# Attention of a diffusion block on one core: units of one key tile for two heads, sums in three of four banks, the bias table reloaded in place

## The reference

```
xn = ln(x, g_norm)
q  = l2norm((xn @ Wq) as 16 heads of 64) * q_scale
k, v = xn @ Wkv;  k = l2norm(k with the null key in front) * k_scale
sim = q @ k.T * 8 + bias[head, i - j]        # bias: a small MLP of the distance i - j
sim = causal mask(sim); attn = softmax(sim)  # the null key is always seen
y   = ln((attn @ v) as 1024 columns @ Wout, g_out)
x   = x + (round(y * 127 / max|y|) / (127 / max|y|)) @ W_ternary.T + bias
```

## Time and profile before

| | |
|---|---|
| time, median of 3 runs | 1911.69 us (1909.09 to 1911.83) |
| span of the profiled execution (its own time is not listed apart) | 1909.3 us |
| busy: PE, DVE, POOL, ACT, PEld | 1637.2, 1605.8, 1329.1, 1167.9, 1088.9 us |
| `score`, L1103, 2560 matmuls | 607.5 us |
| `weigh`, L1125, 8704 matmuls | 601.5 us |
| `bias`, L900, 640 | 697.3 us |
| low part, POOL L479, 448; DVE L910, 192 | 885.9 us; 292.1 us |
| exponential, ACT L611, 640 | 608.9 us |
| DMA | 69.49 MB, 36 GB/s over the span |

### The profile page before, as it was taken

The page is one execution under the profiler, slowest core; times in us unless marked ns, Lnnn a source line. Parts: engine busy times, 40 slices in busy tenths (PEclk is TensorE's granted clock), DMA queues, the critical chain, the costliest instruction groups (busy, mean ns, idle before and its releaser), DMA issues.

```text
span 1909.3 us, 46551 instructions
## 1 busy us (share of the span) xinstructions
PE 1637.2 (86%) x15098; PEld 1088.9 (57%) x15122; DVE 1605.8 (84%) x2569; ACT 1167.9 (61%) x2195; POOL 1329.1 (70%) x806
## 2 busy tenths in 40 slices
PE   3786996988988988988995887889889889889897
PEld 2343553666666666665552554666666666666553
DVE  5885996999999999996664898799999999999576
ACT  1433654777777777777441555677777777777542
POOL 3554675877777777777672676677777778778575
PEclk9997997999999999999997999899999999999998
DMA  5001110001001001000022001000100100100022
GB/s 174 1 0 26 28 56 20 25 24 47 23 26 44 23 31 39 23 23 11 28 71 91 28 27 58 25 25 23 47 23 23 47 23 23 47 23 0 12 72 94
DMA packets 28411, 69.49 MB, mean 36 GB/s; under 512 B 8368, under 2 KB 8880, under 8 KB 24240
## 3 DMA queue, kind: packets, MB, share of 16 engines
q1 hardware_dynamic: 23712, 60.22, 9.9%
q10 hardware_dynamic: 4640, 8.54, 1.3%
HBM read 60.21 MB, written 8.54 MB: 36 GB/s over the span
## 4 chain that ended last, share of the span: by engine, by line
PE 33%; issue 28%; DVE 19%; POOL 16%; DVEq 1%; POOLq 1%; ACT 0%; DMA 0%; ACTq 0%; SPq 0%
PE ps L1103 18%; PE ps L1125 14%; DVE work L900 10%; DVE work L910 6%; POOL rinv L458 3%; POOL work L463 3%; POOL work L490 3%; POOL qo L421 2%; POOL work L508 2%; PE ps L1161 1%; DVE work L926 1%; POOL rstd L453 1%; POOL work L466 1%; POOL work L429 1%; PE ps L1082 0%
## 5 line engine op out<-in xcount | busy, mean ns | idle before, releaser
L479 POOL TENSOR_TENSOR work<-work 128x1024 f16<-128x1024 f32 x448 | 885.9, 1997 | 267.2 <-ACT work L611 261.6
L611 ACT ACTIVATE work<-work 128x1024 f32<-128x1024 f32 (+1 forms) x640 | 608.9, 966 | 296.5 <-DVE work L900 296.4
L900 DVE SCALAR_TENSOR_TENSOR work<-ps,tab 128x1024 f32<-128x1024 f32 (+1 forms) x640 | 697.3, 1110 | 80.1 <-PE ps L1103 77.1
L1103 PE MATMUL ps<-qo,kT 128*128 (+1 forms) x2560 | 607.5, 360 | 115.9 <-DVE work L900 109.3
L1125 PEld LDWEIGHTS ps<-vals,work 128*128 128x128 bf16 (+1 forms) x8704 | 546.3, 98 | 128.8 <-ACT work L611 11.5
L1125 PE MATMUL ps<-vals,work 128*128 128x129 f16 x8704 | 601.5, 220 | 1.9 <-POOL work L479 1.9
L1103 PEld LDWEIGHTS ps<-qo,kT 128*128 128x128 f16 x2560 | 216.4, 98 | 273.2 <-DVE work L900 77.0
L910 DVE TENSOR_TENSOR work<-work 128x1024 f16<-128x1024 f32 x192 | 292.1, 1521 | 0.0
L1071 PE MATMUL ps<-wq,work 128*128 128x512 f16 x768 | 178.0, 390 | 20.5 <-DVE work L829 20.5
L1161 PE MATMUL ps<-wout,work 128*128 128x512 f16 x768 | 172.9, 382 | 0.0
L618 ACT ACTIVATE work<-null_v,p_null 128x65 f32<-128x65 f32 x512 | 135.2, 335 | 9.9 <-DVE work L931 9.9
(11 more groups left out here) (129 smaller groups left out, 1570.6 us busy)
## 6 DMA issues: line engine op xcount, KB each, us to landing
tab<-bias_table SPq DMA_DIRECT2D x32, 1088.0 KB, 5.6
work<-in_x SPq DMA_DIRECT2D x64, 256.0 KB, 2.7
out_x<-work ACTq DMA_DIRECT2D x32, 256.0 KB, 2.8
work<-in_L_cond_Wq SPq DMA_DIRECT2D x1, 2048.0 KB, 12.5
work<-in_L_cond_Wout SPq DMA_DIRECT2D x2, 1024.0 KB, 10.3
qo<-in_L_cond_w SPq DMA_DIRECT2D x1, 1024.0 KB, 8.7
qo<-in_L_cond_b SPq DMA_DIRECT2D x2, 256.0 KB, 4.2
qo<-in_L_cond_g SPq DMA_DIRECT2D x2, 256.0 KB, 4.5
```

Of the source, the lines that this page charges most:

```text
L479: pool.tensor_tensor(low[:, k % LRING, :, c0:512], probs[:, r, :, c0:512], high[:, r, :, c0:512], ALU.subtract).then_inc(low_pool, 1)
L611: act.activation(probs[:, k % RING, :, c0:512], probs[:, k % RING, :, c0:512], ACT.Exp).then_inc(expd, 1)
L900: dve.scalar_tensor_tensor(out=dst, in0=ps[:, 2 * (k % 2):2 * (k % 2) + 2, c0:512], scalar=SCORE, in1=t_ap, op0=ALU.mult, op1=ALU.add).the ...
L1103: last = pe.matmul(ps[:, 2 * (k % 2) + e, c0:512], kT[:, a, j * P:(j + 1) * P], qT[:, bass.ds(h, 1), 512 * i + c0:512 * i + 512].squeeze(1 ...
```

## The change

- A unit is now one key tile for *two heads* (`UNITS`, `unit`): 8 pairs of heads with 40 units, the blocks in the order 3, 2, 1, 0. On the diagonal a unit starts at the tile's own column: 512, 384, 256 and 128 columns. `score` has four matmuls again (two heads, keys' high and low halves); the low halves of odd heads' queries lie before the high ones (`q_part`), the products are all four as before.
- The sums of a block are eight tiles in three banks (3, 3 and 2 tiles), and the blocks go round four banks. A bank is drained as soon as its tiles are complete (`DONE`): q = 0 after the block's last but one unit, q = 1 and 2 after its last. The first `weigh` of a block waits separately for each bank.
- DVE takes 4 low parts of 40, POOL 36.
- `null_part` and `store_o` have eight small copies each, a block being that of two heads.
- The table of a pair of heads is held once; its quarter of 512 columns is loaded again after the block that was the last to use it, and `bias` waits at the units 0, 1, 5 and 9 (`NEARER`).
- PE's loop over heads becomes a written-out one over pairs. The output stage runs over the tiles from the last to the first, and its copy of `x` goes into the table's place.

```diff
-TW = S + P
+TW = S
+NEARER = (0, 1, 5, 9)
 ROUND = 1.5 * 2.0 ** 23
-PAIRS = [(i, q) for i in range(NB) for q in range(2 * i + 2)]
-NP = len(PAIRS)
+HP = H // 2
+BLOCKS = tuple(reversed(range(NB)))
+UNITS = [(i, j) for i in BLOCKS for j in range(4 * i + 4)]
+NU = len(UNITS)
...
-DVE_LOW = (2, 5, 8, 11, 14, 17)
-POOL_LOW = tuple(k for k in range(NP) if k not in DVE_LOW)
-LASTS = {PAIRS.index((i, 2 * i + 1)): i for i in range(NB)}
+DVE_LOW = (4, 10, 22, 32)
+POOL_LOW = tuple(k for k in range(NU) if k not in DVE_LOW)
+SUMS = 3
+SUM_TILES = (range(0, 3), range(3, 6), range(6, 8))
+LASTS = {UNITS.index((i, 4 * i + 3)): i for i in BLOCKS}
+NULLS = {UNITS.index((i, 4 * i + 1)): i for i in BLOCKS}
+DONE = {UNITS.index((i, 4 * i + 2)): (i, (0,)) for i in BLOCKS} | {
+    UNITS.index((i, 4 * i + 3)): (i, (1, 2)) for i in BLOCKS}
+def unit(k):
+    i, j = UNITS[k]
+    return i, j, P * max(0, j - 4 * i)
+def turn(i):
+    return NB - 1 - i
+def sum_bank(i, q):
+    return 4 + (SUMS * turn(i) + q) % 4
...
+        def q_part(u, low):
+            first = qhl[:, u, 0, 0:1]
+            return bass.AP(first.tensor, first.offset + (DH if low else 0),
+                           [first.ap[0], [2 * P, HP], [DH if low else 3 * DH, 2], [1, DH]])
...
-                with sp.Fori(0, H // 2) as h2:
-                    for u in range(2):
-                        h = h2 * 2 + u
-                        sp.wait_ge(biased, (b * H + h - 1) * NP + CB)
-                        sp.wait_ge(tab_ld, 16 * (b * H + h) + 16)
+                with sp.Fori(0, HP) as hp:
+                    for k, i in LASTS.items():
+                        sp.wait_ge(biased, (b * HP + hp - 1) * NU + k + 1 + CB)
+                        sp.wait_ge(tab_ld, 16 * ((b * HP + hp) * NB + turn(i)) + 16)
                         alone(sp)
-                        src = bass.AP(table.tensor, h * TABW + 1, [[1, P], [1, TW]])
-                        sp.dma_start(tab[:, u * TW:(u + 1) * TW], src).then_inc(tab_ld, 16)
-                sp.wait_ge(expd, (b + 1) * H * NP)
+                        src = bass.AP(table.tensor, hp * (2 * TABW) + 1 + P + 512 * i, [[1, P], [TABW, 2], [1, 512]])
+                        sp.dma_start(tab[:, :, 512 * i:512 * i + 512], src).then_inc(tab_ld, 16)
...
-                def null_part(h, i):
-                    n = (b * H + h) * NB + i
-                    act.wait_ge(o_added, n + 1)
-                    for s in range(4):
-                        last = act.activation(null_tmp[:, i % 2, s * VW:(s + 1) * VW], null_v[:, :], ACT.Copy,
-                                              scale=p_null[:, 4 * i + s, bass.ds(h, 1)])
+                def null_part(hp, i):
+                    m = (b * HP + hp) * NB + turn(i)
+                    act.wait_ge(o_added, 3 * m + 3)
+                    for t in range(8):
+                        last = act.activation(null_tmp[:, i % 2, t, :], null_v[:, :], ACT.Copy,
+                                              scale=p_null[:, 4 * i + t % 4, bass.ds(2 * hp + t // 4, 1)])
                     last.then_inc(null_ready, 1)
-                def store_o(h, i):
-                    n = (b * H + h) * NB + i
-                    act.wait_ge(o_rec, n + 1)
-                    act.wait_ge(o_added, n + 1 + 2)
-                    for s in range(4):
-                        last = act.activation(o_all[:, bass.ds(h, 1), 4 * i + s, :].squeeze(1),
-                                              o_sum[:, i % 2, s, :], ACT.Copy, scale=rec[:, i % 2, s:s + 1])
+                def store_o(hp, i):
+                    m = (b * HP + hp) * NB + turn(i)
+                    act.wait_ge(o_rec, m + 1)
+                    act.wait_ge(o_added, 3 * m + 3 + 6)
+                    for t in range(8):
+                        last = act.activation(o_all[:, bass.ds(2 * hp + t // 4, 1), 4 * i + t % 4, :].squeeze(1),
+                                              o_sum[:, i % 2, t, :], ACT.Copy, scale=rec[:, i % 2, t:t + 1])
                     last.then_inc(o_stored, 1)
...
-                def bias(h, k):
-                    n = (b * H + h) * NP + k
-                    i, q = PAIRS[k]
-                    c0 = 256 if k in LASTS else 0
-                    if k == 0:
-                        dve.wait_ge(tab_ld, 16 * (b * H + h + 1) + 16)
+                def bias(hp, k):
+                    n = (b * HP + hp) * NU + k
+                    i, j, c0 = unit(k)
+                    if i == BLOCKS[0] and j in NEARER:
+                        dve.wait_ge(tab_ld, 16 * ((b * HP + hp) * NB + NEARER.index(j) + 1) + 16)
                     dve.wait_ge(scored, n + 1)
                     dve.wait_ge(pv_done, n + 1)
-                    dst = probs[:, k % RING, :, c0:512]
-                    t_ap = tab[:, bass.ds((h % 2) * TW + (512 * i - 256 * q + c0), 2 * P)]
-                    t_ap = bass.AP(t_ap.tensor, t_ap.offset, [t_ap.ap[0], [P, 2], [1, 512 - c0]])
-                    dve.scalar_tensor_tensor(out=dst, in0=ps[:, 2 * (k % 2):2 * (k % 2) + 2, c0:512],
-                                             scalar=SCORE, in1=t_ap, op0=ALU.mult, op1=ALU.add
+                    x0 = 512 * i - P * j + c0
+                    dve.scalar_tensor_tensor(out=probs[:, k % RING, :, c0:512],
+                                             in0=ps[:, 2 * (k % 2):2 * (k % 2) + 2, c0:512], scalar=SCORE,
+                                             in1=tab[:, :, x0:x0 + 512 - c0], op0=ALU.mult, op1=ALU.add
                                              ).then_inc(biased, 1)
-                def low_part(h, k):
-                    n = (b * H + h) * NP + k
-                    c0 = 256 if k in LASTS else 0
+                def low_part(hp, k):
+                    n = (b * HP + hp) * NU + k
+                    i, j, c0 = unit(k)
                     r = k % RING
                     dve.wait_ge(expd, n + 1)
                     dve.wait_ge(pv_done, n + 1 + RING - LRING)
                     dve.tensor_tensor(low[:, k % LRING, :, c0:512], probs[:, r, :, c0:512], high[:, r, :, c0:512],
                                       ALU.subtract).then_inc(low_dve, 1)
-                def drain(h, i):
-                    n = (b * H + h) * NB + i
-                    last = PAIRS.index((i, 2 * i + 1))
-                    z = 4 + 2 * (i % 2)
-                    dve.wait_ge(pv_done, (b * H + h) * NP + last + 1 + RING)
-                    dve.wait_ge(null_ready, n + 1)
-                    dve.wait_ge(o_stored, n + 1)
-                    acc = ps[:, z:z + 2, 0:2 * VS].rearrange("p z (s d) -> p z s d", d=VS)
-                    null = null_tmp[:, i % 2, :].rearrange("p (z s d) -> p z s d", z=2, d=VW)
-                    part = o_part[:, i % 2, :, :].rearrange("p (z s) d -> p z s d", z=2)
-                    total = o_sum[:, i % 2, :, :].rearrange("p (z s) d -> p z s d", z=2)
-                    dve.tensor_tensor(denom[:, i % 2, :].rearrange("p (z s) -> p z s", z=2), acc[:, :, :, 2 * DH],
-                                      null[:, :, :, DH], ALU.add).then_inc(o_den, 1)
-                    dve.tensor_tensor(part, acc[:, :, :, DH:2 * DH], null[:, :, :, 0:DH], ALU.add
-                                      ).then_inc(o_low, 1)
-                    dve.wait_ge(o_den, n + 1)
-                    dve.reciprocal(rec[:, i % 2, :], denom[:, i % 2, :]).then_inc(o_rec, 1)
-                    dve.wait_ge(o_low, n + 1)
-                    dve.tensor_tensor(total, acc[:, :, :, 0:DH], part, ALU.add).then_inc(o_added, 1)
-                def head(h, first):
-                    for k in range(NP):
-                        bias(h, k)
+                def drain(hp, k):
+                    i, done = DONE[k]
+                    m = (b * HP + hp) * NB + turn(i)
+                    dve.wait_ge(pv_done, (b * HP + hp) * NU + k + 1 + RING)
+                    if 0 in done:
+                        dve.wait_ge(null_ready, m + 1)
+                        dve.wait_ge(o_stored, m + 1)
+                    for q in done:
+                        t0, n = SUM_TILES[q].start, len(SUM_TILES[q])
+                        acc = ps[:, sum_bank(i, q), 0:n * VS].rearrange("p (t d) -> p t d", d=VS)
+                        dve.tensor_tensor(denom[:, i % 2, t0:t0 + n], acc[:, :, 2 * DH],
+                                          null_tmp[:, i % 2, t0:t0 + n, DH], ALU.add).then_inc(o_den, 1)
+                        dve.tensor_tensor(o_part[:, t0:t0 + n, :], acc[:, :, DH:2 * DH],
+                                          null_tmp[:, i % 2, t0:t0 + n, 0:DH], ALU.add).then_inc(o_low, 1)
+                        if q == 2:
+                            dve.wait_ge(o_den, 3 * m + 3)
+                            dve.reciprocal(rec[:, i % 2, :], denom[:, i % 2, :]).then_inc(o_rec, 1)
+                        dve.wait_ge(o_low, 3 * m + q + 1)
+                        dve.tensor_tensor(o_sum[:, i % 2, t0:t0 + n, :], acc[:, :, 0:DH], o_part[:, t0:t0 + n, :],
+                                          ALU.add).then_inc(o_added, 1)
```

(80 more changed lines are left out.)

102 lines of the change are left out of this document (55 added, 47 removed).

## The result

The changed kernel takes **1993.33 us** (median of 5 runs, 1990.1 to 2002.39) where the kernel before takes 1911.67 (5 runs, 1909.09 to 1911.83): 4.4% slower, ratio **1.0439, interval 1.0417 to 1.0460**. The forecast was 1930, with a range up to 1970. The direction was right, the size was not: 82 us instead of 18.

A forecast was written before the change was run, and what follows sets the result against it. PE was taken as the bound, 62.3 of 71.2 us per pair, the rest held by a late DVE. Then 60.6 + 10.2 + 1.8 = 72.6 us per pair, +9 per batch, +18 in all: 1930 us, range 1890 to 1970.

The forecast's parts named there:

- one clock for the whole sum: All PE prices in the attention were taken at TensorE clock 1.00 (2.4 GHz), with no term for a lower clock.
- Block-end wait: PE, first weigh after a block, waits for DVE's drains: 2.55 us each, four per pair, 10.2 us.
- PE gets to tile 3 later than 2 us: Stated sign of being wrong: at a block end PE reaches tile 3 over 2 us after score(L+5).
- DVE's low parts: DVE's four low parts per pair: those at units 12 and 24 delay PE's score 0.9 us each, 1.8 per pair.
- Engines: Expected busy time per pair of heads in the profile after: DVE near 55 us, POOL near 62.
- PE's floor: PE's score and weighing matmuls per pair of heads: falls from 62.3 to 60.6 us.
- the remaining 8.9 us: In the kernel before, the part of a 71.2 us pair beyond PE's 62.3 us, called PE held by DVE.
- Code: PE's written-out heads: code streaming costs 0; rival, not hidden: +90 us, 2020 us, chance 0.04.
- Edges: Per batch: last two block ends behind the last score −5.1 us, remaining weighs +1.9, output stage copies +1.
- POOL's shadow: Rival: POOL is late, block-end waits cost nothing, a pair takes about 66.5 us: 1836 us, chance 0.12 in part or whole.
- Dearer low parts: Rival: four DVE lows delay PE 1.2 us each, ACT's copies 1.6 per pair: 77.2 a pair, 2004 us, chance 0.15.
- Short block-end waits: Rival: drains early enough that a block end costs one 0.8 us wait: 65.6 us a pair, 1820 us, chance 0.04.

The follow-up runs named there:

- filled kernels: Changed kernel with useless matmuls in PE's waits at each block end: six in the second wait 1920.87 us, three in the second 1923.31, three in the first 1923.07.
- half filled wait: Changed kernel with three useless 512-column matmuls on PE in the second wait of each block end: 1923.31 us, ratio 1.0057.
- without DVE's low parts: Changed kernel with DVE's drains one unit earlier and DVE_LOW = (), so POOL does all 40 low parts of a pair: 1802.34 us, ratio 0.9426.
- early drains: Changed kernel with DVE draining q = 0 right after bias(L+4), q = 1 before bias(L+5) and q = 2 after it: 1800.25 us, ratio 0.9423.
- loop version: Changed kernel with PE's attention as a loop over pairs of heads again, the first pair before it: 2009.88 us, ratio 1.0523.

## Why the prediction was right in sign and wrong in size

**The step that failed: one clock for the whole sum.** The sum was made "with the TensorE clock at 1.00", read from the earlier trace rows; every PE price was taken at it, and no rival moved it. The sum thus put the clock's loss at nothing. The change makes PE stop twice within 3 us at each block end, and the clock falls behind most of them. From the filled kernels: 71.9 us a pair with the waits and without the falls, 78.3 with four falls, 76.9 with three; 1993.3 − 1921 to 1923 = **70 to 72 us of the 82**. Checked in another way: 3.4 us at half speed delay up to 1.7 us of matmuls, and the pairs give (78.3 − 71.9) / 4 = 1.6 and (76.9 − 71.9) / 3 = 1.7. The two profiles of the changed kernel give 1.7, and 43 falls at 1.6 to 1.7 are 69 to 73 us.

The profile before could have warned a little: the clock does fall in this kernel, in the stages around the attention (0.93 from 890 to 1200 us of the span), while the sum put four new pairs of stops into each pair of heads. Its attention alone, at 1.00 with waits of up to 1.8 us, gave no warning. The Trainium skill, page "TensorE: Matmul & The Clock Gate", section "A second HAM failure mode: psum-queue depth-cycling", tells of a kernel in which short idle times between groups of matmuls, where accumulator banks are handed round, make the clock swing between its two levels. The windows of 0.50 and 0.51 here agree. It spoke against this change, without a price, and the prediction did not weigh it.

**Nearly right, at constant clock, and in part by luck.** The forecast for a pair was 72.6 us; the kernel with the half filled wait has 71.9. Point by point:
- *Block-end wait.* PE was to stand at tile 6 at 3.98 us after `score(L+5)`: 4.06 measured. The two waits were announced "near 0.8 and 1.8": 0.78 and 1.53. Four block ends come to 9.1 us where 10.2 was forecast. Their count, some 62, is right. The sign of being wrong "PE gets to tile 3 later than 2 us" contradicts the prediction's own 2.1; measured are 2.2 (473.92 to 476.13).
- *DVE's low parts.* Two delays of 0.9 a pair were forecast, 1.8 us; there is one, of 0.81.
- *Engines.* DVE "near 55": 55.65. POOL "near 62": 59.09. It collides less than assumed. In the full group without DVE's low parts a subtraction takes 1898 ns, as the 1.89 of the earlier trace rows.
- *PE's floor.* 60.6 us was forecast; 62.0 is measured: 71.9 less 9.1 and 0.8 of waits in the kernel with the half filled wait (its matmuls take the place of waiting), and 63.7 less 1.7 with early drains. The kernel before shows the same gap: the prediction called "the remaining 8.9 us" of 71.2 PE held by DVE, but the earlier trace rows have 6.9, so some 2.0 us of the pair were in no term. The waits and the low parts were forecast 2.1 us too long and the floor 1.4 too short; that these cancel to 0.7 is luck. What fills the gap was not looked for.
- *Code.* Priced at 0; the loop version is no faster, and nothing shows a cost of the code.
- *Edges.* Without falls the whole is +9 to +12 us, of which 16 × 0.7 = 11 are the pairs, so the edges together are near 0 where −4.5 was forecast. One is dearer: the output stage. Timelines of ACT and PE after the last `bias`, which is at 936.72 (compare):

```profile
941.69 1.04 ACT L686 CAST work<-qo 128x1024 f16<-128x1024 f32 x1 [0.17 <-ACT qo L658]
...
945.07 1.59 PE L1179 MATMUL ps<-ident,work 128*128 128x128 f16 x16 [4.02 <-POOL work L521]
```

  945.07 − 936.72 = 8.35 us against 897.45 − 890.6 = 6.9: +1.5 where +1 was forecast.

**The rivals.** POOL's shadow did not come: POOL waits 13.0 us a pair for ACT. Dearer low parts gave the nearest number (2004) for a reason that is not there; the right total of a rival is no support for it. Code is excluded by the loop version. "Short block-end waits" (1820) came to nothing in this kernel, but describes the early-drain one: 1800.

**What the change would have been worth.** Fewer low parts on DVE alone give the old kernel 5.3%. In the changed kernel that gain is there (PE's wait for `bias` fell by 6.1 us a pair) and is spent twice: 9.1 us a pair on the block-end waits, and 5.0 to 6.4 on the clock that they bring down.

**Open.** Why some block ends are not followed by a fall was not found: the waits of those 11 are as long as the others. So it is also open what decides how many falls an execution has, 43 or 49, and why the loop kernel has more. The fastest kernel was not taken further.

## What to carry to other kernels

When a change adds stops to TensorE, write the clock into the sum as a term of its own: a stop costs its length and, if it is long or others stand close to it, what the matmuls behind it lose at 1.2 GHz; here 10 us of net waiting became 82. If sums share banks, place the drain a whole step ahead of its reader on DVE's queue; counting both queues out gave these waits to about a tenth (10.2 us a pair against 9.1). And before a restructuring that is to relieve an engine, try the one constant that relieves it: here it had 102 us of the 110 that the best kernel reached.
